# Another order of maxima, scores and contexts on TensorE in the attention steps of a block with routed experts

## The reference

```python
h = _layernorm(x, axis=-1) * (1 + ca) + sa
x = x + ga * _L0_attn_ref(h, Wq, Wk, Wv, Wo)      # 16 heads of width 8
h = _layernorm(x, axis=-1) * (1 + cb) + sb
x = x + gb * _L0_ffn_ref(h, ...)                  # 8 experts, the best 2 of each token
...
scores = jnp.einsum('bhqd,bhkd->bhqk', q, k) / math.sqrt(hd)
attn = jax.nn.softmax(scores, axis=-1)
ctx = jnp.einsum('bhqk,bhkd->bhqd', attn, v)
```

## Time and profile before

| | |
|---|---|
| median of three runs | 934.29 us (932.97 to 938.32) |
| profiled execution, its own time | 933.2 us |
| its span, first to last instruction | 931.4 us |
| busy: PE, PEld, DVE, ACT, POOL | 852.5, 372.8, 753.1, 756.7, 403.0 us |
| exponentials | 1024 of 597 ns |
| reductions of a maximum unit | 512 of 1216 ns |
| chain that ended last | PE 67%, DVE 9%, POOL 7% |

### The profile page before, as it was taken

One profiled execution on the slowest core, in us unless ns is written; L12 is line 12 of the kernel. 1 busy time (PEld: TensorE's weight loads), 2 busy tenths in 40 slices (PEclk: granted clock), 3 DMA queues, 4 the chain that ended last, 5 costly groups with the idle time before them and its releaser, 6 DMA issues.

```text
span 931.4 us, 22099 instructions
## 1 busy us (share of the span) xinstructions
PE 852.5 (92%) x7998; PEld 372.8 (40%) x7998; DVE 753.1 (81%) x1039; ACT 756.7 (81%) x1639; POOL 403.0 (43%) x679
## 2 busy tenths in 40 slices
PE   6577999999999999999999999999999799898982
PEld 3322222222232223223322322332233299898982
DVE  7797999999989989998998899899885046733387
ACT  6634999999998999989989899998989866565661
POOL 8576236300013731640373055036414545577574
PEclk9887999999999999999999999999999989999997
DMA  5543444414121000540101011010000122223453
GB/s 147 199 174 137 155 172 155 166 58 155 46 112 36 8 30 25 149 149 2 35 2 36 2 52 63 4 36 2 2 2 14 44 58 60 63 70 88 127 142 115
DMA packets 60394, 72.06 MB, mean 77 GB/s; under 512 B 9949, under 2 KB 42212, under 8 KB 60288
## 3 DMA queue, kind: packets, MB, share of 16 engines
q1 hardware_dynamic: 55456, 61.82, 20.3%
q0 software_dynamic: 4544, 8.44, 2.6%
q10 hardware_dynamic: 288, 0.40, 0.2%
HBM read 30.08 MB, written 41.06 MB: 76 GB/s over the span
## 4 chain that ended last, share of the span: by engine, by line
PE 67%; DVE 9%; POOL 7%; issue 4%; ACT 3%; DMA 3%; SPq 2%; DVEq 0%; POOLq 0%
PE ps_ctx L890 26%; PE ps_scores L875 16%; PE ps_max L854 10%; DVE half_max L1100 7%; PE ps_max L1915 4%; PE ps_scores L1925 4%; ACT probs L1002 3%; PE ps_scores L911 2%; POOL y_rows L1708 2%; POOL slots L1363 2%; POOL route_xn_attend L1275 1%; SPq L1671 1%; DMA v<-slots 1%; POOL h L1285 1%; POOL route_xn_attend L1280 1%
## 5 line engine op out<-in xcount | busy, mean ns | idle before, releaser
L1100 DVE TENSOR_REDUCE half_max<-ps_max 128x2 f32<-128x1024 f32 x512 | 597.3, 1216 | 55.0 <-PE ps_max L854 51.8
L1002 ACT ACTIVATE probs<-ps_scores 128x512 f32<-128x512 f32 x1024 | 553.7, 597 | 51.5 <-PE ps_scores L875 35.0
L890 PE MATMUL ps_ctx<-probs,v_grp 128*32 128x256 f32 x4096 | 328.8, 393 | 14.4 <-ACT probs L1002 13.2
L854 PE MATMUL ps_max<-k_set,q_set 48*128 48x512 bf16 x1024 | 204.6, 384 | 12.5 <-DVE half_max L1100 11.1
L875 PE MATMUL ps_scores<-q_set,k_set 51*128 51x512 bf16 x1024 | 212.9, 389 | 1.9 <-DMA q_set<-max_rows 1.6
L890 PEld LDWEIGHTS ps_ctx<-probs,v_grp 128*32 128x32 f32 x4096 | 81.1, 108 | 193.7 <-issue 101.3
L875 PEld LDWEIGHTS ps_scores<-q_set,k_set 51*128 51x128 bf16 x1024 | 56.5, 93 | 211.5 <-ACT probs L1002 175.0
L1739 ACT ACTIVATE probs<-ps_max,v 128x128 f32<-128x128 f32 x312 | 88.9, 368 | 50.3 <-PE ps_max L1915 50.3
L1708 POOL DMA_INDIRECT y_rows<-probs,v x78 | 90.9, 1166 | 59.8 <-DVE probs L1788 39.9
L733 POOL CAST max_parts<-row_max 128x16 bf16<-128x16 f32 x32 | 6.3, 196 | 240.9 <-DVE row_max L1108 240.6
L1915 PE MATMUL ps_max<-probs,v 128*128 128x128 f32 x624 | 85.3, 281 | 2.6 <-DVE v L1768 2.6
(11 more groups left out here) (220 smaller groups left out, 652.6 us busy)
## 6 DMA issues: line engine op xcount, KB each, us to landing
slots<-zero_rows SPq DMA_DIRECT2D x43, 387.0 KB, 4.8
q_terms<-parts SPq DMA_DIRECT2D x24, 256.0 KB, 2.5
k_terms<-parts SPq DMA_DIRECT2D x24, 256.0 KB, 3.0
q_set<-q_terms SPq DMA_DIRECT2D x32, 192.0 KB
k_set<-k_terms SPq DMA_DIRECT2D x32, 192.0 KB
v<-slots SPq DMA_DIRECT2D x78, 64.5 KB, 1.9
q_set<-max_rows SPq DMA_DIRECT2D x128, 3.0 KB
w_all<-in_we SPq DMA_DIRECT2D x1, 2048.0 KB
```

The costliest lines, as they stand in the source:

```text
L854: ins = pe.matmul(ps_max[n % 2][:, r * BANK:(r + 1) * BANK], q_set[g % SETS][rows, u, tile * P:(tile + 1) * P], k_set[g % SETS][rows, u, c ...
L890: ins = pe.matmul(ps_ctx[32 * head:32 * head + 32, columns], v_grp[g % 2][:, tile, head, :], probs[:, s % RING, head, columns], start=tile ...
L1002: act.activation(probs[:, s % RING, place, :], ps_scores[n % BANKS_S][:], ACT.Exp, scale=float(HD) ** -0.5).then_inc(slot_taken, 1)
L1100: dve.reduce_max(half_max[tile // HT % 2][:, c, 2 * u:2 * u + 2, tile % HT], ps_max[n % 2][:].rearrange("p (r n) -> p r n", r=2), axis=AX. ...
```

## The change

In `step` of TensorE's program the first maximum unit moves ahead of the first pair of scores and the second unit ahead of the second pair. A step was half context, pair, unit, half context, pair, unit; it is now half context, unit, pair, half context, unit, pair. The last step of each chunk keeps its order: half context, pair, half context, unit, pair, unit. Nothing is added or taken away, and the other engines' programs are the same.

```diff
@@ -915,19 +915,20 @@
             def step(s):
 
                 first, second = units(s)
+                last = s % NT == NT - 1
                 add_ctx(s, 0)
+                if first is not None and not last:
+                    max_scores(first)
                 if s + 1 < ALL_STEPS:
                     scores(s + 1, 2)
                     scores(s + 1, 3)
-                if first is not None and s % NT < NT - 1:
-                    max_scores(first)
                 add_ctx(s, 1)
-                if first is not None and s % NT == NT - 1:
-                    max_scores(first)
+                if first is not None:
+                    max_scores(first if last else second)
                 if s + 2 < ALL_STEPS:
                     scores(s + 2, 0)
                     scores(s + 2, 1)
-                if first is not None:
+                if first is not None and last:
                     max_scores(second)
                 for what, n in beside(s):
                     if what == "negated":
```

## The result

The changed kernel takes **950.8 us** in the median (949.7 to 958.1, four runs), the kernel before 933.6 beside it: 1.9% slower, the ratio 1.0191 with a 95% interval of 1.0166 to 1.0216. Forecast were 950.5 and a range of 945 to 957. The profiled execution's span grew from 931.4 to 947.9.

The account below looks back on a forecast made before the run. TensorE's own order was taken as full, setting the 2.22 us step. Thirty chunks at +0.71 gave +21.3, less 5.1 taken back: +16.2 on 934.3, forecast 950.5, range 945 to 957.

Parts of the forecast that it names:

- The chain and the plain step: Step with units: half context to unit 0.57, unit to pair 0.23, pair through ScalarE's exponentials to next context 1.55; +0.13.
- The places in a chunk: Per regular chunk: six steps, including first and fourth, +0.13 each, fifth -0.12, last +0.05; +0.71 in all.
- What takes some back: Places where something other than TensorE's order sets the step: together -5.1, with 0 and -10 as ends.
- (a): Steps with VectorE's extra routing work, statistics and choices: -0.4 and -0.3 in each of three batches, -2.1.
- (b): TensorE's wait for GpSimd's h ahead of the transposes, three times: the steps ahead arrive 0.4 later, -1.2.
- (c): TensorE's single 1.6 wait for rows of maxima behind a queue of weight loads: -1.1.
- (d): Steps with router and projections, where exponentials or banks are late already: 0.3 given back per batch net, -0.9.
- The start: The first two steps: VectorE sets them and the pair now stands behind their last unit, +0.2.
- VectorE does not pace the plain steps: Denies the rival that VectorE's 2.26 sets plain steps and nothing is lost: 936, 5 in 100.
- The faster case: Rival: units reach VectorE 0.23 earlier, so TensorE's 16.2 us of weight-load waits for VectorE go: 920, 3 in 100.
- My sign for it: Sign named for units reaching VectorE earlier: TensorE's waits for VectorE, 16.2 us between 200 and 700 us, get smaller.
- Nothing absorbed: Rival: exponentials' wait also adds in VectorE's and GpSimd's stretches, +21.3 stands: 955.6, or 963 if fifth steps pay; 10 in 100.

Follow-up runs that it names:

- the cut exponentials: Exponentials from the fourth step on taken of 256 of 512 columns, in the changed kernel (926.4 us) and in the kernel before (923.3 us).
- the single moves: Against the kernel before, only the first unit moved ahead of its pair: 957.1 us; in another kernel only the second: 957.9 us.
- the second attempt at a faster order: Kernel before, with first unit ahead of pair only in fifth steps, and both exponentials ahead of ScalarE's context copy at chunk ends: ratio 0.9979.

## Why the prediction was right, point by point

**The chain and the plain step.** Forecast 2.35, C1 to Ma 0.57, Ma to Pa 0.23, Pa to C1 1.55: each as measured, within 0.01. The 16 steps without units had shown the chain bare, and the change put one unit into it. That the chain through ScalarE is the cause is shown by the cut exponentials; the single moves rule out a price of the order itself, but they ran into the bank's chain, which the prediction counts at single places of a chunk only. TensorE's own sum for the new order is 2.22 and not 2.24, as the cut exponentials show too; nothing hung on that.

**The places in a chunk.** First and fourth step +0.13 each (2.94 and 2.52 for 2.80 and 2.38), fifth -0.13 (forecast -0.12), last +0.05, the chunk +0.71, as forecast to the hundredth.

**What takes some back.** Each chunk's first contexts give it, against the 0.71 of a regular one. (a) Chunks with statistics +0.31, with choices +0.40: -0.40 and -0.31, forecast -0.4 and -0.3. (b) The wait for GpSimd: its chunk +0.25, so -0.46, forecast -0.4. (c) The wait for the rows of maxima has gone from 1.6 to

```profile
PE ps_scores L875 <- DMA q_set<-max_rows: 0.5, 1, 0.5
```

and its chunk to -0.29, so -1.00, forecast -1.1. That the queue took the same time in both executions is partly luck: from its first weight load to the pair that waits it took 23.3 before and 23.2 after, but 21.7 to 24.0 over all the kernels here, and the second attempt at a faster order, with steps hardly changed, waited only 0.2. (d) **This step failed.** Router and projections were to give back 0.3 a batch; their three chunks changed by +0.70, +0.82 and +0.77, together 0.16 a batch more than a regular chunk. Before, such a matmul stood directly behind a unit, which covered it, as in the first projection's step:

```profile
266.19 0.38 PE L854 MATMUL ps_max<-k_set,q_set 48*128 48x512 bf16 x2
266.51 1.15 PE L1595 MATMUL ps_scores<-wo,parts 128*128 128x128 f32 x8
```

Now it pays the chain and the second wait: +0.20 and not +0.13 a step. The term is mis-sized by 0.46 a batch, 1.4 us in all. With the second wait taken away the three chunks change by +0.70, +0.71 and +0.65, so that wait is half of it, 0.23 a batch. The other half is lateness that I had counted on and that these steps did not have; in which of them is open.

**The start.** I called the first two steps VectorE's and added 0.2 for them. They are not: TensorE ran them at the lower of its two clock levels, 1.2 GHz, and in the profiled execution after it left that level earlier. So the clock of the kernel before was not full all through the steps, as I had written; it was from about 91 us on. Stretches 84 to 88 and 88 to 92 us, before and then after (clock third from the end):

```profile
84.00:88.00 4.00, 4.00 (x28) 0.71 (x32) 1.26 (x2) 2.33 (x5) 3.92 (x4) 0.50 0.37 137
88.00:92.00 4.00, 4.00 (x32) 0.68 (x28) 2.65 (x3) 2.21 (x6) 3.86 (x3) 0.57 0.17 66
```

```profile
84.00:88.00 4.00, 4.00 (x26) 0.67 (x24) 2.45 (x2) 2.17 (x4) 3.92 (x3) 0.50 0.52 199
88.00:92.00 4.00, 3.94 (x40) 1.02 (x36) 3.63 (x4) 3.23 (x6) 3.79 (x4) 0.97 0.00 0
```

The second step takes 3.03 for 3.80 by that, and the first context came 1.15 earlier, in a part that the change does not touch. Behind the attention the lower level comes in other places (0.79 for 0.57 in one stretch, 0.72 for 1.00 in another) and gives 1.5 back the other way. From the third step to the last one with units the change costs **+17.0**; with -1.9 ahead of it and +1.5 behind, that is the 16.5 of the spans. My sum from the same step on was 15.7: 21.3 less 5.3, and less the 0.26 that the 21.3 holds for the first two steps. It was 1.2 short, by (d) and small things.

**How close the number came.** The medians differ by 17.1, where the sum said 16.2. That 950.8 stands within 0.3 of 950.5 is luck in part: the kernel before took 933.6 in these runs, 0.7 less than the 934.3 that the forecast started from.

**The rivals.** VectorE does not pace the plain steps: its reductions have 10 us more idle time, and with short exponentials both orders run at 2.22, under the 2.26 that two reductions need, since the chunk's end makes it up. The faster case: units now arrive earlier, and nothing came of it. My sign for it was badly chosen. I wrote that TensorE's waits for VectorE would shrink; the same view as the earlier trace rows, here from 200 to 715 us, and who VectorE waited for, now say

```profile
DVE half_max L1101 <- PE ps_max L854: 49.6, 60, 1.9
...
PEld ps_max L854 <- DVE half_max L1101: 40.8, 89, 1.2
```

40.8 us for 16.2, while chunks with VectorE's extra work lost less time than the others. The row counts idle time of the queue of weight loads ahead of a unit. Behind a half context that queue is idle for some 0.4, whoever ends it (272 such waits of a unit, 111.9 us, have no releaser in that view); before, the pair stood there. The step lengths decide, not this row. Nothing absorbed: refuted by (a) to (c).

## What to carry to other kernels

When two engines hand work to and fro, write down for each hand-over how much time the waiting engine's other work covers, and reorder only where the cover stays longer than the chain. Here 0.09 us of spare decided: moving both units broke the context's chain, and moving either alone broke the bank's. Look for a stretch of the same kernel that lacks the cover (a tail, a first step), since it shows the bare chain, and the price of an order can be read there before it is tried. Banks that are freed by the same engine are a second chain with a deadline of its own; count it too.

## What the runs showed of the hardware

A matmul that waits for two things has one of the waits in a sequencer instruction of its own, 51 ns long, ahead of it. It starts later where that wait is the one that ends last: the projection by 0.10, counted from its pair (0.54 for 0.44). The first context of a chunk waits for the copy and for exponentials and shows both cases. What the sequencer holds ahead of the context at 221.71 in the kernel before, and ahead of that at 221.91 in the second attempt at a faster order (the last two times are its first and last start):

```profile
L888 PEldq EVENT_SEMAPHORE  x1: 51/51/51, 221.2 to 221.2; - x1
```

```profile
L888 PEldq EVENT_SEMAPHORE  x1: 51/51/51, 221.8 to 221.8; - x1
```

Each stands right behind the end of the copy (221.16 and 221.76), so it is the copy's wait that the sequencer holds. In the first kernel the exponential ends later, and the context starts 0.05 after it, like a C1 with one wait; in the second the copy ends last, and the context starts 0.15 after it. No run takes that wait away. The Trainium skill (Perfetto Trace Analysis, Identifying Dependency Chains) notes that instructions that wait on several engines may have EventSemaphore instructions put ahead of them; this trace agrees, also where both waits are for the same engine, and shows what it costs.

At the full granted clock a pair of scores and a unit follow each other at 0.22 to 0.23, a context follows either at 0.31 to 0.32, and either follows a context at 0.57 to 0.58, in whatever order they stand: TensorE's own time for a step was 2.22 in both orders where nothing waited.
